# A DLRM tower on one core: the looped kernel against an unrolled one with a ring of fourteen quads

## The reference, cut to what matters

```python
e = jnp.stack([tbl_0[ids[:, 0]], ..., tbl_31[ids[:, 31]]], axis=1)   # [2048, 32, 256]
dots = jnp.einsum('bnd,bmd->bnm', e, e)
z = dots[:, iu, ju]                                                  # upper triangle: [2048, 496]
h = jnp.concatenate([z, dense_ctx], axis=1)                          # [2048, 512]
h = jnp.maximum(h @ W_top1 + b_top1, 0.0)                            # 512 -> 512
h = jnp.maximum(h @ W_top2 + b_top2, 0.0)                            # 512 -> 256
y = h @ W_top3                                                       # 256 -> 1
```

## Time and profile before

| | us |
|---|---|
| time before, median of 3 runs | 655.48 (654.58 to 655.81) |
| span of the profiled execution | 903.1 |
| busy in the profile: PE matmul / PE weight load | 615.7 / 581.2 |
| busy in the profile: DVE / ACT / POOL | 311.3 / 264.5 / 459.0 |
| idle of ScalarE ahead of its copies of the dots, releaser unknown ("remote") | 310.5 |

### The profile page before, as it was taken

The page is one execution under the profiler, slowest core; times in us unless marked ns, Lnnn a source line. Parts: engine busy times, 40 slices in busy tenths (PEclk is TensorE's granted clock), DMA queues, the critical chain, the costliest instruction groups (busy, mean ns, idle before and its releaser), DMA issues.

```text
span 903.1 us, 11558 instructions
## 1 busy us (share of the span) xinstructions
PE 615.7 (68%) x4416; PEld 581.2 (64%) x4416; DVE 311.3 (34%) x674; ACT 264.5 (29%) x497; POOL 459.0 (51%) x486
## 2 busy tenths in 40 slices
PE   1032776877768687777747978487787778688793
PEld 1032775776767676766747968377686767677693
DVE  0070432433325242252323523144332623243441
ACT  1010322423223241242314323133332423243431
POOL 6667155655545565345554464465556455565100
PEclk9996788888968888787978878789897979889797
DMA  5633023242312423124231332225223242224000
GB/s 129 212 81 108 24 77 94 83 76 71 94 58 76 82 81 88 55 66 84 82 93 55 54 106 71 75 80 77 70 82 89 67 83 82 83 82 71 24 1 0
DMA packets 36190, 69.28 MB, mean 77 GB/s; under 512 B 15788, under 2 KB 20300, under 8 KB 36172
## 3 DMA queue, kind: packets, MB, share of 16 engines
q0 software_dynamic: 23040, 62.95, 27.9%
q1 hardware_dynamic: 13132, 6.08, 2.7%
HBM read 68.98 MB, written 0.01 MB: 76 GB/s over the span
## 4 chain that ended last, share of the span: by engine, by line
PE 35%; another core or an unknown queue 32%; ACT 10%; issue 9%; DVE 8%; DMA 3%; SPq 2%; ACTq 0%; DVEq 0%
PE gram_ps L293 17%; PE tr_ps L272 6%; ACT dots L438 6%; PE gram_ps L322 5%; PE gram_ps L331 4%; DMA row_numbers<-in_table_row_numbers 3%; ACT emb_t L427 3%; DVE onehot L507 3%; PE sel_ps L352 3%; DVE dots_t L450 2%; SPq L200 2%; PE gram_ps L311 2%; DVE packed L462 1%; DVE emb_t L427 1%
## 5 line engine op out<-in xcount | busy, mean ns | idle before, releaser
L242 POOL DMA_INDIRECT rows<-in_tbl,ids_sb x480 | 458.3, 955 | 379.5 <-PE tr_ps L272 199.3
L293 PE MATMUL gram_ps<-emb_t 128*128 128x124 f32 x2048 | 283.2, 303 | 130.7 <-ACT dots L438 42.9
L293 PEld LDWEIGHTS gram_ps<-emb_t 128*128 128x128 f32 x2048 | 271.9, 216 | 142.5 <-issue 77.4
L438 ACT COPY dots<-gram_ps 32x124 f32<-32x124 f32 x256 | 93.2, 364 | 404.0 <-remote 310.5
L438 DVE COPY dots<-gram_ps 32x124 f32<-32x124 f32 x256 | 94.1, 368 | 317.7 <-remote 248.7
L272 PE MATMUL tr_ps<-ident,rows 128*128 128x128 f32 x960 | 143.8, 300 | 76.5 <-DVE emb_t L427 38.3
L272 PEld LDWEIGHTS tr_ps<-ident,rows 128*128 128x128 f32 x960 | 122.9, 156 | 85.0 <-issue 80.2
L427 ACT COPY emb_t<-tr_ps 128x512 f32<-128x512 f32 (+1 forms) x128 | 127.8, 1063 | 88.7 <-issue 46.2
L427 DVE COPY emb_t<-tr_ps 128x512 f32<-128x512 f32 (+1 forms) x128 | 126.6, 1050 | 67.8 <-PE tr_ps L272 36.4
L352 PE MATMUL sel_ps<-onehot,sel_high 125*128 125x256 f32 x256 | 77.7, 327 | 9.7 <-issue 9.4
L352 PE MATMUL sel_ps<-onehot,sel_low 125*128 125x256 f32 x256 | 74.3, 314 | 9.4 <-issue 9.0
(11 more groups left out here) (18 smaller groups left out, 82.0 us busy)
## 6 DMA issues: line engine op xcount, KB each, us to landing
rows<-in_tbl,ids_sb POOLq DMA_INDIRECT x480
sel_ids<-in_ids_by_field SPq DMA_DIRECT2D x16, 125.0 KB
emb_t<-in_tbl SPq DMA_DIRECT2D x2, 1000.0 KB
w_sb<-in_W_top SPq DMA_DIRECT2D x1, 1024.0 KB
w_sb<-in_W_top SPq DMA_DIRECT2D x1, 512.0 KB
ids_sb<-in_ids SPq DMA_DIRECT2D x16, 16.0 KB
packed<-in_dense_ctx SPq DMA_DIRECT2D x16, 8.0 KB
out_y<-y_sb SPq DMA_DIRECT2D x8, 1.0 KB
```

Source lines behind the costliest of these rows:

```text
L242: pool.indirect_dma_start(out=rows[c][:, f - c * CHUNK, :], out_offset=None, in_=tables[f], in_offset=bass.IndirectOffsetOnAxis(ap=ids_sb[ ...
L293: last = nc.tensor.matmul(gram_out[fill % 2][:, g, :], four.rearrange("p s f -> p (s f)"), four[:, :, 0:firsts], start=(h == 0), stop=(h = ...
L438: last = copy(of_fill.rearrange("p f g -> p g f"), gram_out[who][own, :, s * firsts:(s + 1) * firsts])
```

## The change

The kernel is written anew without loops, with the same split into gathered and selected fields and the same arithmetic per tile.

- `places`, `quads`, `rows_landed`: the fields are put in a new order, the gathered ones first and 27 and 31 last, and the rows of W_top1 are permuted to fit. A tile's 30 gathered fields are 7 quads of four and one of two.
- The buffers of gathered rows are a ring of 14 quads (`RING`), 56 fields, in place of four buffers of 8 fields. Quad g waits for the transposes of quad g - 14.
- The first two tiles gather all 32 fields (484 gathers in all), so no selection is needed for them; `select` runs for 7 pairs, one field per tile (`jobs`), 14 times 32 matmuls by the profile's count (records), where it was 16 times.
- All ids are loaded at the start in two transfers. A table comes as 8 KB rows in two transfers.
- The high part of a table is made by ScalarE (`high_table`) and the low part by VectorE (`split_table`), a table at a time, between the copies of tile 0. Before, both were VectorE's and came ahead of its copies.
- `period(t)` replaces `step`: on TensorE a quad's transposes stand ahead of each two fills of the gram. The selection stands between quad 4 and the turn (or before layer 3 if there were more of them). Each PSUM hand-over has a semaphore of its own.

```diff
-CHUNK = 8
-BUFFERS = 2
+RING = 14
+SPRAY = 16
...
+    def quads(t):
+        return fields // QUAD if t < PAIR else -(-(fields - n_sel) // QUAD)
...
+    early = n_sel // 2
+    def jobs(t):
+        p, at = (t + 1) // PAIR, range(0, early) if t % PAIR else range(early, n_sel)
+        return [(p, i) for i in at] if 1 <= p < tiles // PAIR else []
...
-        rows = [sbuf(f"rows{c}", [P, CHUNK, width]) for c in range(chunks)]
+        rows = [sbuf(f"rows{r}", [P, QUAD, width]) for r in range(RING)]
...
+            sp.dma_start(ids_sb[:, 0, :], ids[0:P, :]).then_inc(ids_loaded[0], DMA)
+            sp.dma_start(ids_sb[:, 1:tiles, :], ids[P:batch, :].rearrange("(t p) f -> p t f", p=P)
+                         ).then_inc(ids_loaded[1], DMA)
...
+                table = tables[f].rearrange("(p c) w -> p (c w)", c=SELECT_CHUNKS)
+                sp.dma_start(sel_raw[0:sprayed_rows, n, :], table[0:sprayed_rows, :]).then_inc(tables_loaded[n], DMA)
...
-            with pool.Fori(1, tiles // BUFFERS) as p:
-                for u in range(BUFFERS):
-                    for c in range(chunks):
-                        gather_chunk(p, u, c)
+            for g, (t, k) in enumerate(every_quad):
+                if k == 0 and t < 2:
+                    pool.wait_ge(ids_loaded[t], DMA)
+                wait(pool, transposed[1], g - RING + 1)
+                for j, place in enumerate(places(t, k)):
+                    f = order[place]
+                    pool.indirect_dma_start(
+                        out=rows[g % RING][:, j, :], out_offset=None, in_=tables[f],
+                        in_offset=bass.IndirectOffsetOnAxis(ap=ids_sb[:, t, f:f + 1].bitcast(u32), axis=0),
+                    ).then_inc(rows_loaded[g % RING], DMA)
...
+            def period(t):
+                turning = (lambda k: transpose(t, k)) if t < tiles else (lambda k: None)
+                now = jobs(t)
+                for k in range(fills_each):
+                    turning(k)
+                    gram(t - 1, 2 * k)
+                    gram(t - 1, 2 * k + 1)
+                turning(4)
+                for job in now[:1]:
+                    select(*job)
+                turn(t - 1)
+                turning(5)
+                if t == 1:
+                    pe.wait_ge(weights_loaded, 5 * DMA)
+                layer1(t - 1)
+                turning(6)
+                layer2(t - 1)
+                turning(7)
+                for job in now[1:]:
+                    select(*job)
+                layer3(t - 1)
...
+            for k in range(quads(0)):
+                emb_copy(dve, 0, copy, 0, k)
+                if k >= 4 and k - 4 < n_sel:
+                    split_table(k - 4)
```

More of the change, by code:

```diff
@@ L29 @@
 QUAD = 4
-CHUNK = 8
-BUFFERS = 2
+PAIR = 2
 DMA = 16
@@ L34, with field_order @@
 SELECT_CHUNKS = 8
+RING = 14
+SPRAY = 16
+def field_order(fields):
+    return [f for f in range(fields) if f not in SELECTED] + list(SELECTED)
 def squares(fields):
@@ L298, in all_copied, with gram @@
-            def all_copied(t, fills):
+            def gram(t, fill):
+                u, k, turn_of_bank = t % PAIR, fill % 2, fill // 2
+                if fill == 0:
+                    for h in range(D_HALVES):
+                        pe.wait_ge(emb_copied[h], quads_before[t + 1])
+                    for b in range(2):
+                        wait(pe, sel_copied[b][u], jobs_in_bank(b, t // PAIR))
+                if turn_of_bank:
+                    pe.wait_ge(dots_copied[k], t * fills_each + turn_of_bank)
+                elif k == 0:
+                    wait(pe, y_copied, t)
+                else:
+                    wait(pe, hid2_copied[1], t)
+                for g in range(bank_groups):
+                    s = (fill * bank_groups + g) * QUAD
+                    for h in range(D_HALVES):
+                        four = emb_t[u][:, h, s:s + QUAD, :]
+                        last = nc.tensor.matmul(gram_out[k][:, g, :], four.rearrange("p s f -> p (s f)"),
+                                                four[:, :, 0:firsts], start=(h == 0), stop=(h == D_HALVES - 1))
+                last.then_inc(gram_done[k], 1)
@@ L300, in all_copied, with turn @@
+            def turn(t):
                 for k in range(2):
-                    wait(pe, mlp_copied[k], t * FILLS[k] + min(fills, FILLS[k]))
-            def turn(t):
-                all_copied(t, 0)
-                for k in range(2):
+                    pe.wait_ge(dots_copied[k], (t + 1) * fills_each)
                     pe.wait_ge(packed_ready[k], t + 1)
@@ L398, in _ @@
-            pe.wait_ge(ident_ready, 1)
-            for c in range(chunks):
-                for q in range(quads):
-                    transpose_quad(0, 0, c, q)
-                if c == 1:
-                    pe.wait_ge(tables_split, 1)
-                if c > 1:
-                    for part in range(4):
-                        select(0, c - 2, part)
-            pe.wait_ge(weights_loaded, 5 * DMA)
-            step(1, 1, 1)
-            with pe.Fori(1, tiles // BUFFERS - 1) as p:
-                step(p * BUFFERS, 0, p)
-                step(p * BUFFERS + 1, 1, p + 1)
@@ new lines, in _, with emb_copy @@
+            pe.wait_ge(ident_ready, 1)
+            for k in range(quads(0)):
+                transpose(0, k)
+            for t in range(1, tiles + 1):
+                period(t)
+        def emb_copy(eng, h, copy, t, k):
+            if t >= tiles or k >= quads(t):
+                return
+            g, at = quads_before[t] + k, places(t, k)
+            eng.wait_ge(transposed[h], g + 1)
+            copy(emb_t[t % PAIR][:, h, :, at[0]:at[-1] + 1].rearrange("p (g s) f -> p f s g", s=QUAD),
+                 tr_ps[h][g % 2][:, 0:len(at), :].rearrange("p f (s g) -> p f s g", s=QUAD)
+                 ).then_inc(emb_copied[h], 1)
@@ L586 @@
+            for k in range(quads(0)):
+                emb_copy(act, 1, copy, 0, k)
+                if k >= 3 and k - 3 < n_sel:
+                    high_table(k - 3)
+            act.wait_ge(tables_split, n_sel)
+            for t in range(1, tiles + 1):
+                if t == 1:
+                    act.wait_ge(weights_loaded, 5 * DMA)
+                period(t)
 def kernel(**inputs):
```

540 lines of the change are left out of this document (225 added, 315 removed).

## The result

The changed kernel takes 659.63 us (median; 656.86 to 662.05 in 20 runs). The kernel before took 655.64 in the same comparison (median of 20 runs). The ratio is 1.0054, with a 95% interval of 1.0035 to 1.0073: **slower by 4 us**, where 3.5 us less had been predicted.

What follows compares the result with a forecast made beforehand. GpSimd's issue of gathers was taken as the bound: 615.65 + 1.85 + 38.23 gave 655.7 before. The change took 3.7 off GpSimd's chain and added 0.3 at the end: 655.5 - 3.4 = 652.1, stated as 652.0, range 638 to 660.

Steps and rivals of the forecast that it cites:

- Gathers bound the kernel at 1.25 us each: GpSimd: its issue of gathers, 1.25 us each, sets the pace; 480 before, 484 after, 605 us.
- Ids of tile 1, 5.45 us: GpSimd at the start: the wait for tile 1's ids behind the tables goes, saving 5.45 us.
- Tables, 3.2 us: GpSimd's gathers beside VectorE's two table subtractions: 3.2 us longer together, bounds 0 and 4.4.
- Ring, two selections fewer, no loops: nothing: A deeper ring, less selection on TensorE and unrolled code: worth nothing; about 33 instruction packets, hidden in TensorE's spare 3.5 us.
- A quad's transposes ahead of each two fills, +0.3: TensorE, last gather to last gram: about 2.1 us where 1.85 stood, so plus 0.3, bounds 0 and 3.
- the predicted -3.7: GpSimd's chain to the end of its last gather slot: 611.9 after the change against 615.65 before.
- list of signs of being wrong: Changed profile: pace other than 1.25, transposes waiting for rows long after issue, last gram at clock 0.50, time under 640.
- Landing of about nothing: End of the chain: the last gather's landing, with what lies around the span, comes to about nothing and is carried unchanged.
- The rival on the slower side: TensorE's clock falls to half level at the end, two to four fills at +1.9: 656 to 660 us; chance 0.15.
- Gathers slow only under the profiler: GpSimd's gathers are faster unprofiled, 1.20 or 0.95 us each: time 600 to 645 us; chance 0.10.
- the 73% of one row: GpSimd at the start: a gather lengthened by 3.2 us beside a subtraction of 4.42 us, a share applied to both halves.

Runs made afterwards that it cites:

- a_nostore: The changed kernel with only the last pair's results stored, the outputs of pairs 0 to 6 left out: 657.32 us, 1.0003 of before.
- before, second profile: The kernel before, unchanged, profiled again beside the follow-up runs: 655.19 us, span 653.4.
- a_copy: The changed kernel again, unchanged, on the chip of the runs that leave out single stores: 660.47 us, 1.0064 of before.
- a_row: The changed kernel with layer 3 turned round, so y is stored as one contiguous row of 256 words: 650.67 us, 0.9895 of before.
- b_row: The kernel before with layer 3 turned round, so y is stored as one contiguous row: 648.95 us, 0.9884 of before.
- the disturbed one: The execution of the kernel before, unchanged, that was profiled for the prediction: span 903.1 us, where the runs take 655.48.
- b_nostore: The kernel before with only the last pair's results stored, the outputs of pairs 0 to 6 left out: 656.13 us, 0.9985 of before.
- a_sel3: The changed kernel with y stored as one row, two fills ahead of each quad's transposes, three selected fields, ring of 11 quads: 634.89 us, 0.9672 of before.
- experiment 7, a_row_ring11: The changed kernel with y stored as one row and a ring of 11 quads in place of 14: 649.19 us, 0.9901 of before.
- experiment 2: Both kernels with only the last pair's results stored: the changed one 657.32 us (1.0003 of before), the one before 656.13 us (0.9985).
- a_skip6: The changed kernel without the store of pair 6 alone, the other seven stores kept: 656.80 us, 0.9996 of before.

## Why the prediction was wrong

From the end of the last gather on, a span has two parts: up to the last gram, and from there to the end. In us, from the profiles (the last column is the time of the profiled execution, 1.8 us more than the span, 2.2 in a_nostore; the predicted 652.1 was reckoned from the median of 655.5, so it is 0.1 less than its parts):

| | last gather ends | to the last gram | to the end | time |
|---|---|---|---|---|
| predicted, before / after | 615.65 / 611.9 | 1.85 / 2.1 | 38.2 / 38.2 | 655.7 / 652.1 |
| before, second profile | 612.4 | 3.7 | 37.3 | 655.2 |
| changed | 612.0 | 9.5 | 38.1 | 661.4 |
| a_copy | 612.0 | 8.0 | 37.6 | 659.4 |
| a_nostore | 611.8 | 4.4 | 36.8 | 655.1 |
| a_row | 613.7 | 5.0 | 30.7 | 651.1 |
| b_row | 612.4 | 4.0 | 30.8 | 649.0 |

Each row is one execution, and runs of one kernel spread over 3 to 9 us, so a difference of a microsecond between two rows shows little. The first column is firmer: in all 12 profiles with two selected fields, the disturbed one left out, the last gather ends between 611.8 and 613.7 us, whichever kernel it is (b_nostore 612.9, a_row 613.7).

- *Gathers bound the kernel at 1.25 us each.* Right, in every profile. a_sel3 has 14 gathers fewer, 17.5 us by this pace, and the medians give 15.7 (650.63 to 634.89).
- *Ids of tile 1, 5.45 us.* The mechanism was right (the changed kernel has no such wait), the size was not: in the second profile of before the slot ahead of 43.77 is 3.21 us long where an ordinary one is 1.25, so 2.0 and not 5.45. This term was read from the disturbed execution. Before, GpSimd ends at 612.4 and not at 615.65, and of the predicted -3.7 about -0.4 is left. This error made a gain out of no change; by itself it would have given a tie and not a loss.
- *Tables, 3.2 us.* Measured 1.9 + 1.9 = 3.8, within the bounds.
- *Ring, two selections fewer, no loops: nothing.* Right for the ring (experiment 7); 35 packets of instructions came where 33 had been estimated. b_row against a_row shows that all of it together brings nothing that can be measured.
- *A quad's transposes ahead of each two fills, +0.3.* **This is the step that failed.** It said "New is that TensorE waits for rows with a gram queued behind", and then took each row to land in time, as the sum had carried the landing "unchanged". The store of `y` makes gathers issued beside it land 8.1 to 8.5 us after their issue (the two of experiment 2) where the median is 2.8, and the place of that store had not been looked at. The prediction's own list of signs of being wrong had this one, transposes that wait for rows long after they were issued. Before, four fills cover tile 15's rows. In the changed kernel nothing stands there, and TensorE, which has only about 3 us of waits in a tile to regain it (3.42 in a_nostore), still has most of the lag at the end. Measured: +4.3 and +5.8 us in two profiles (a_copy and the changed kernel). The two errors together, 3.3 us of gain that was not there and 4.0 to 5.5 of lag that was not counted, make 7.3 to 8.8 us; the predicted -3.4 and the measured +4.0 lie 7.4 apart. Without the word-wise stores the order costs 0.6 (a_nostore 4.4, b_nostore 3.8) or 1.0 (a_row 5.0, b_row 4.0). The 3.8 of a_row_ring11 shows that single profiles scatter by as much, so the predicted 0.3 is neither borne out nor refuted.
- *Landing of about nothing.* The 655.48 had been reached by errors that cancelled: 3.3 too much in GpSimd's end and 0.9 in the tail against 1.9 too little up to the last gram and 1.8 around the span that were not counted. That the sum met the median was luck, and did not show that its terms were right.
- *The rival on the slower side* gave 656 to 660, and 659.63 lies in it, but by the clock, so this was luck. Fills at 5.09 and layer 1 at 5.36 us do show the half level in period 15, and layer 1 (3.74 in a_copy) is the whole difference between the changed kernel's 9.5 and a_copy's 8.0. But a_skip6 has its two fills at 5.44 and its layer 1 at 5.32 us, its last gram follows the last gather after 4.9 us, and it is not slower than before. The slow stretches stand behind waits of TensorE, though not behind every one (layer 1 took 5.36 us after a wait of 2.65 ahead of the turn and 3.74 in a_copy after one of 2.66); they are not what separates the two kernels. *Gathers slow only under the profiler*: the same 15.7 us speak against it, since 14 gathers at 0.95 would be at most 13.3.

## What to carry to other kernels

A store of one kilobyte, word by word, cost this change about 4 us: look at the shape of each small store, and at what the engine with the next wait has queued, since the price depends on whether work stands in front of that wait. A lag that is made up in the middle of a kernel costs nothing there, but one that arises in the last tile is paid for the most part (5.8 us at that tile's first transposes and 5.4 at its gram, the changed kernel against a_nostore); one edit that removes it there is worth as much as removing it everywhere. And where the profiled execution is far from the timed ones, its start-up waits may not be taken as terms.

## What the runs showed of the hardware

- The store of 128 x 2 single words takes as long alone at the end (8.0 us in the changed kernel from its issue to the end of the span) as beside the gathers (from issue to landing 7.5 to 10.6, median 8.4, over all eight); the same 1 KB as one row takes 1.5 at the end. In packets the changed kernel has 34423 and a_row 32263, 270 more for each of the eight stores, with the same 70.03 MB. The Trainium skill, "DMA: Bandwidth & Descriptors" (Specifications), says that a transfer needs 512 bytes or more to reach the line rate, and that below this the engine reads, modifies and writes. The trace agrees as far as the time goes (52 GB/s at a share of 0.79); what the engine does inside no run here shows.
- Gathers issued beside this store land after up to 9.4 us in the changed kernel (those issued from 200 to 208 us), where the median of all is 2.8. The store is not the only thing that does this: the first six gathers of a_nostore and of a_row, issued while the tables are loaded, land after 8.6 to 9.5 us as well. The same page of the Trainium skill (Queues, rings and completion order) says that each engine takes turns between its queues packet by packet. The late gathers fit turns with a slow partner, but no run here tells this from another way of sharing.
- A gather that begins during one of VectorE's instructions on the tables ends 0.8 us after that instruction does, wherever it began: in the changed kernel at 34.63 behind a subtraction that ends at 33.82, and at 41.50 behind one that ends at 40.70; in a_sel3 at 37.41 behind 36.60; in the second profile of before at 45.88 behind a cast that ends at 45.07. All 14 profiles have it so, within 0.80 to 0.83 us, the disturbed one too. A gather that was under way when the subtraction began is not longer (a_sel3, at 34.14: 0.95 us). So the price is no fixed share of the subtraction, as the prediction took it, but about the time that is left of it: 1.9 us where the gather began 0.23 us into it, 1.1 where it began 1.09 us into it. The Trainium skill, "SBUF — State Buffer" (SBUF: two separate sides, the box on the "DVE blocks DMA" trap), says that GpSimd can't write descriptors while VectorE is in an operation that takes the shared port, and names the fp32 copy. The trace agrees for the cast, and shows the same for the subtraction of two tiles, of which the box does not speak. The prediction had set this aside for the 73% of one row.
